# Gathers of a block's rows in four groups of eight, each group issued when the group ahead has landed

## The reference, cut to what matters

```python
out = einsum('bsi,io->bso', Efou * ys[:, None, :], weight) * d[:, None, :]      # xf: 4096 x 512
gate_probs = softmax(xf @ gate_w.T)
top1 = argmax(gate_probs, axis=-1)
one_hot = one_hot(top1, N_ROUTING)
masked = xf[None, :, :] * one_hot.T[:, :, None]
h = relu(einsum('end,edh->enh', masked, w1) + b1[:, None, :])                   # hidden: 2048 wide
expert_out = einsum('enh,ehd->end', h, w2) + b2[:, None, :]
shared = relu(xf @ sw1 + sb1) @ sw2 + sb2
return x + expert_out.sum(axis=0) + shared
```

## Time and profile before

| | |
|---|---|
| median of 3 runs | 1473.6 us (1469.45 to 1476.79) |
| profiled execution, its own time | 1470.11 us |
| its span, first to last instruction | 1468.4 us |
| TensorE clock granted, mean over the span | 0.97 |
| PE busy | 1377.6 us (94%) |
| DVE busy | 1004.7 us (68%) |
| ACT busy | 679.7 us (46%) |
| POOL busy | 370.3 us (25%) |

### The profile page before, as it was taken

The page is one execution under the profiler, slowest core; times in us unless marked ns, Lnnn a source line. Parts: engine busy times, 40 slices in busy tenths (PEclk is TensorE's granted clock), DMA queues, the critical chain, the costliest instruction groups (busy, mean ns, idle before and its releaser), DMA issues.

```text
span 1468.4 us, 17361 instructions
## 1 busy us (share of the span) xinstructions
PE 1377.6 (94%) x5990; PEld 1131.1 (77%) x5990; DVE 1004.7 (68%) x1424; ACT 679.7 (46%) x988; POOL 370.3 (25%) x328
## 2 busy tenths in 40 slices
PE   9999999997699695996999999999999999897998
PEld 8888888886488574875888888888888887686886
DVE  7988978673499573864647787878698867535332
ACT  4365645453265351653656544444565454322220
POOL 0000006366237435062000000000000112355785
PEclk9999999999799897997999999999999999999999
DMA  6958584966477465563366888878987899998753
GB/s 220 303 180 243 199 260 167 271 212 236 151 257 267 157 245 164 202 232 110 132 229 218 274 271 268 273 262 254 293 252 228 272 288 310 284 316 188 220 164 40
DMA packets 243449, 334.54 MB, mean 228 GB/s; under 512 B 71760, under 2 KB 106576, under 8 KB 243088
## 3 DMA queue, kind: packets, MB, share of 16 engines
q1 hardware_dynamic: 216592, 299.58, 62.0%
q0 software_dynamic: 21248, 30.30, 9.3%
q10 hardware_dynamic: 5520, 3.54, 0.8%
HBM read 201.25 MB, written 149.29 MB: 239 GB/s over the span
## 4 chain that ended last, share of the span: by engine, by line
PE 58%; DMA 7%; another core or an unknown queue 4%; issue 4%; DVE 2%; ACT 1%; POOL 1%; SPq 0%; ACTq 0%; DVEq 0%; POOLq 0%
PE bank L2088 27%; PE bank L2010 22%; PE bank L2117 7%; DMA hin<-hidden_scratch 3%; DMA hin<-expert_hidden 1%; DMA y_rows<-x_rows,tab 1%; DMA out<-y_rows,tab 1%; DVE hl L1477 1%; PE bank L2029 0%; DMA y_rows<-sorted_rows_out 0%; PE bank L2130 0%; ACT hl L1035 0%; DVE vb L1510 0%; DMA hidden_scratch<-vt 0%
## 5 line engine op out<-in xcount | busy, mean ns | idle before, releaser
L2010 PE MATMUL bank<-xw,w_hi 128*128 128x512 f32 x1792 | 564.0, 396 | 66.0 <-ACT vb L1059 26.9
L2010 PEld LDWEIGHTS bank<-xw,w_hi 128*128 128x128 f32 x1792 | 341.5, 191 | 143.6 <-ACT vb L1059 29.2
L2088 PE MATMUL bank<-hl,w_hi 128*128 128x512 f32 x1344 | 414.4, 389 | 2.9 <-DVE hl L1477 2.8
L1477 DVE TENSOR_TENSOR hl<-hin,hl 128x512 fp32r<-128x512 f32 x400 | 265.8, 689 | 197.4 <-ACT hl L1035 179.7
L1035 ACT CAST hl<-hin 128x512 fp32r<-128x512 f32 x400 | 245.7, 624 | 320.8 <-PE bank L2088 184.6
L2010 PE MATMUL bank<-xw,w_lo 128*128 128x512 f32 x896 | 353.7, 395 | 0.1
L2088 PEld LDWEIGHTS bank<-hl,w_hi 128*128 128x128 f32 x1344 | 251.9, 188 | 56.9 <-issue 2.8
L2088 PE MATMUL bank<-hl,w_lo 128*128 128x512 f32 x672 | 261.5, 389 | 0.0
L2010 PEld LDWEIGHTS bank<-xw,w_lo 128*128 128x128 f32 x896 | 171.2, 191 | 36.5
L1059 ACT ACTIVATE vb<-bank,b 128x512 f32<-128x512 f32 x192 | 129.0, 689 | 150.5 <-PE bank L2010 91.4
L880 POOL DMA_INDIRECT rows<-xf_scratch,quad_tab x128 | 138.0, 1078 | 152.8 <-DVE xw L1446 112.4
(11 more groups left out here) (199 smaller groups left out, 1330.3 us busy)
## 6 DMA issues: line engine op xcount, KB each, us to landing
hin<-hidden_scratch SPq DMA_DIRECT2D x168, 512.0 KB
hidden_scratch<-vb SPq DMA_DIRECT2D x120, 512.0 KB
hidden_scratch<-vt SPq DMA_DIRECT2D x48, 512.0 KB
hin<-expert_hidden SPq DMA_DIRECT2D x32, 512.0 KB
w_new<-w_shared SPq DMA_DIRECT2D x52, 256.0 KB, 4.4
expert_hidden<-vb SPq DMA_DIRECT2D x24, 512.0 KB
ring<-x_cols SPq DMA_DIRECT2D x32, 256.0 KB
xf_scratch<-xo SPq DMA_DIRECT2D x32, 256.0 KB, 4.6
```

The lines of the kernel that those rows point to most:

```text
L1477: nc.vector.tensor_tensor(hl[:, n % HL, 1, :], hin[:, n // 2 % LOADS, n % 2, :], hl[:, n % HL, 0, :].bitcast(F32), ALU.subtract).then_inc( ...
L2010: last = nc.tensor.matmul(up_bank(u, UP_BANK[c])[p][:], w[:, DOWN_W[c], pair, part], xw[:, c, x, k, :], start=(c in FRESH and n == 1), sto ...
L2088: last = nc.tensor.matmul(bank[p][:], w[:, DOWN_W[c], i, part], hl[:, n % HL, h, :], start=(i == 0 and q == 0), stop=(i == PAIRS - 1 and q ...
```

## The change

In `gather_rows`, ahead of places 8, 16 and 24, POOL waits until the eight gathers of the part before have landed. The number of gathers, their order, addresses, destinations and semaphores stay. No other engine's program changes. The waits come four times three, since there are four gathers.

```diff
                 pool.wait_ge(xw_lo, STEPS * s)
                 for j in range(JW):
+                    if j > 0 and j % (JW // FLIPS) == 0:
+                        pool.wait_ge(rows_sorted[j // (JW // FLIPS) - 1], DMA * JW // FLIPS * (s - BLOCKS + 1))
                     if (s - 1) * GROUPS == LOOSE_UP[0] and j == JW // FLIPS:
                         pool.wait_ge(loose_up_done, 2)
                     u, a = (s - BLOCKS) * JW // W + j // W, j % W
                     pool.indirect_dma_start(rows[:, j, :], None, xf_dram,
                                             bass.IndirectOffsetOnAxis(quad_tab[:, a, u:u + 1], 0)).then_inc(rows_sorted[j // (JW // FLIPS)], DMA)
```

## The result

The changed kernel takes 1424.87 us (median of 4, 1423.46 to 1429.34). The kernel before, beside it, takes 1471.53 us (median of 4, 1468.08 to 1476.79). The ratio is 0.9685, 95% interval [0.9646, 0.9724]: 3.2% faster.

A forecast was written before the change was run, and what follows sets the result against it. PE was taken as the bound, stalled in four gathers by its completion word arriving late. From 1470.1 us, - 81.2 + 26 + 13.6 = - 41.6 gives 1428.5, stated as 1430 us; range 1392 to 1490.

The forecast's parts named there:

- the late word: In the four gathers, PE's word that a product is done reaches ACT and DVE 12 to 18 us late.
- the late part: Part 3 of a block's gathered rows, with pauses landing 68.6 us after block start; DVE wants it at 61.2, 7.4 late.
- What is removed: Excess of the four slow groups lying in the gathers over 19.1 us each: 81.2 us, all forecast to go.
- stay under all of these: Claim that runs of eight gathers are shorter than runs seen before lateness, so the late word was costed at nothing.
- What is added: Loss from the late part 3: 26 us of PE waiting plus 13.6 us of clock over four blocks.
- A pause: POOL's wait for landing, three per gather: taken as 3.0 us, adding 2.7 us each and 8.1 us a gather.
- The bounds of 1.4 and 5.5 us: Pause lengths from a sorted-row gather and a scatter to memory; with gathers of 41.7 and 47.3 us, 1389 and 1480 us.
- PE standing: PE waits behind the late part 3: 6.5 us a block after 0.9 us of slack, 26 us in all.
- The clock: Clock lost after four more PE idle stretches, 3.4 us each from one 4.9 us stretch: 13.6 us.
- the prediction's chain: Part 3 wanted at 61.2 us, then DVE's fixed chain to group 3's additions; PE needs the third, about 0.9 us slack.
- The slower rival: Held words come free only after some 4 us of POOL quiet, so pauses free nothing: 1483 to 1502 us; chance 0.22.
- The rival that the gathers do not make the stall: Something simultaneous stalls PE, and the 8.1 us of longer gathering stay hidden: 1470 us, give or take 5; chance 0.12.

## Why the prediction was right where it was measured

It said 1430 us and got 1424.87. What it said of the gain came true: the pauses keep the late word small enough that PE does not stand for it. What it said of the loss came true as far as the late part; the step from there to PE was another. With the runs above both sides of its sum can be checked one at a time.

**What is removed: 81.2 us, right in size.** On the chips with the late word, the kernel before takes 1470.3 to 1477.1 us; without gathers it takes 1391.5 on one of these, with plain DMAs 1388.1 to 1389.1, and on the chip without the late word 1389.3 to 1390.7. From the 1471.5 us beside the first result down to 1389.3 that is 82.2 us. The changed kernel removes nearly all: it is 1424.9 - 1423.6 = 1.3 us slower with the late word than without, inside the spread of its runs.

The way there had errors. It read the lateness as 12 to 18 us by pairing a waiting instruction with the wrong product. `add` waits for a count of `up_mm`: DVE's addition at 384.98 waits for the product whose last matmul was issued at 355.72, so its word was 28.9 us late, and what ACT took at 359.02 was an earlier product. And runs of eight do not "stay under all of these". In the first gather of before, the run of matmuls that ended when ten gathers were out was told 6.9 us late. In the third, one was told 2.5 us late eight gathers after the pause, and thirteen gathers, not eleven, go out from 546.15 to 561.54. That eight was short enough is measured; the reason given for it was partly luck.

**What is added: 39.6 us, measured 34.3.** By terms, first on the chip of the result, then on the third:

- A pause was taken as 3.0 us; it is 3.8 and 3.3 us (means of 12 each). The bounds of 1.4 and 5.5 us hold both means.
- PE standing was put at 26 us, 6.5 a block; it is 23.4 and 24.5 us.
- The clock was put at 13.6 us, 3.4 a block; it is 7.9 and 9.2 us. This term was mis-sized. 12.00 x (1 - 0.72) takes the lost clock over the idle stretch too. The window has 23 matmuls, and 84 take 19.1 us at full clock, so they are worth 5.2 us of the 7.11 that PE was busy: 1.9 us of clock, and 7.6 for four (an estimate from these rows).

The second term is near for the wrong reason. In block 3, part 3 is turned at 396.44, 13.0 us after the fourth group began at 383.4. By the prediction's chain 4.8 us are free (61.2 + 0.9 - 57.3), so PE would have lost 8.2 us there; it stood for 6.07. The step behind part 3 was wrong: the prediction let PE wait for the third of DVE's additions behind the turn. The trace shows ACT's first high half, which waits for all four turns and stands ahead of four bank takes. Reordering that half and what follows took the loss out of the fourth groups. That a later part and a shorter chain gave nearly the loss that was forecast is luck.

**The slower rival** (the word stays held until POOL is quiet for some 4 us) is refuted: nine pauses of 1.6 to 3.4 us are enough, and with the changed kernel no group before the fourth is over 23.3 us, where the rival had 33 to 46.

**The rival that the gathers do not make the stall** is refuted on the two chips that have it, by the three kernels without indirect gathers, and for a reason it is half right. The gathers alone do not make it: on the third chip the same run of 32 goes by unnoticed. There the rival would have been right on the mechanism and wrong on the time: it hid the longer gather behind the stalled groups. Without stalled groups the pauses cost their full 34 us. The Trainium skill, "SBUF — State Buffer", section on who interferes with whom, says that a DMA never contends with a compute engine and that PE never waits on anyone. It says so of the ports into SBUF. The third chip agrees: with rows in order, the groups of blocks 3 to 6 take 19.0 to 21.1 us. On the other two there are four groups of 32 to 47 us, but what is late there is PE's semaphore, by up to 28.9 us, and PE stands for banks that ACT or DVE could not take in time. The section does not speak of that, so the prediction leaned on it for more than it says.

**What the prediction did not see.** It took the 81 us for a property of the program. They are a property of the program on some chips, or of these chips at the time: of the three chips on record, two had it and one, tried twice, did not. Had the kernels first been compared on the third, the same change would have been 2.4% slower, and the sum without its first term, 39.6 us, would have been the forecast, 5 us from the 34.3 measured.

**What stays open.** Why the word comes late was not found; the traces of both kinds of chip show POOL's issues at the same pace. One difference shows even without a stall: on the two chips the record of `up_mm` has gaps in every kernel, 8 to 10 increments where there is no late word (plain DMAs or none), and on the third it has none. What loses records may or may not be what delays the word. Whether it is the indirect form as POOL works it out or the scattered rows is open, since both runs with rows in order fell on the chip that has no late word. Whether the difference lies in the chip itself or in its state that day can't be told from one visit or two to each. Whether a slower pace without any pause would do was not separated either.

## What to carry to other kernels

When nobody is busy and a signal arrives late, ask first whether the stall exists on another chip; a remedy with a cost of its own can change sign there. Prefer a remedy that costs nothing when the disease is absent: holding the gathers back by the progress of the engine that suffers gave 4.6% (1402.8 against 1470.3 us) on a chip with the stall. The same waits, with ACT's first high half freed as well, were level (1389.7 against 1390.7 us) on the chip without it. Waiting for landings costs 3.3 to 3.8 us each time here. Before adding such a pause, follow what is late at its far end through each engine's order, for the instruction that stops PE may only stand ahead of the one that it needs.

## What was not expected of the hardware

- The same program takes 1389.3 to 1390.7 us on one chip and 1470.3 to 1477.1 us on two others, each steady within 0.6% from run to run.
- On those two, PE's word that a product is done (the increment of its semaphore) comes up to 28.9 us late during runs of indirect gathers of 64 KB, issued 1.25 us apart. The first late words come when eight to twenty-three gathers of a run are out. What was held then arrives together, 0.08 us apart.
- Sixty-four plain DMAs from POOL in a row, with the DMA engines 0.95 busy, do not bring it about. Pauses after every eight, 3.8 us long in the mean, leave 2.7 us of lateness at most; nine pauses of 1.6 to 3.4 us in four gathers leave 4.5 us.
